# Fetches of a layer's first chunks wait for blocks of queries (graph transformer and message passing, one core)

## The chip, the cores and the metric

One core of one Trainium2 chip runs the whole program. The metric is the time of one execution on the device in microseconds; the median of three runs of the kernel before is 5631.02 us (5628.84 to 5631.04). The engines are PE (matrix products), DVE (vector), ACT (scalar functions), POOL (which here issues the indirect fetches) and SP (which issues plain transfers).

## The reference, cut to what matters

3125 nodes with 64 features, 100000 edges, sorted by destination. First four layers of attention along the edges, width 128, eight heads of 16:

```python
q = (h @ Wq.T + bq)[dst]; k = (h @ Wk.T + bk)[src]; v = (h @ Wv.T + bv)[src]   # per edge, 8 heads
alpha = sum(q * k) / 4                     # one number per edge and head
ex = exp(alpha - segment_max(alpha, dst)[dst])
out = segment_sum(ex / segment_sum(ex, dst)[dst] * v, dst)
h = layer_norm(gate(out, h @ Ws.T + bs) + h);  h = gelu(h @ W1.T + b1) @ W2.T + b2 + h
```

Then the result, added to x and normalised, goes through one stage of message passing: for every edge the products of x[src] and x[dst] and 16 radial functions of its length go through a small network, messages are summed by destination, and a second small network with a norm gives the output of 3125 x 64.

## The kernel before

**Nodes** are held in NB = 25 blocks of 128 rows, in NI = 5 groups of BW = 5 blocks. **Edges** are laid out in 806 places of 128 edges; a place belongs to one block of destinations. Sixteen places are a chunk (CH = 16), in four groups of four places (NG = 4, G = 4). There are 51 chunks in a pass; the last has 6 places. The fetched rows of a chunk lie in one of RING = 4 slots of SBUF, so that at most four chunks are fetched ahead. There are five passes over the edges: four layers and the message stage.

**A layer's head.** At the end of the layer in front (or in setup, for layer 0) PE and DVE make keys and values for all blocks (`keys` L953, `projected_keys` L1452, counted in `a_ev`), and SP writes them to the table `kv_table` in five transfers (`store_table` L389, counted in `tab_out`). Then PE makes queries: for each block one product of 128 x 256 and one transpose (`queries` L960, lines L966 and L970), and DVE evicts the block with a bias (L1464), which counts `q_ev` up by one; PE's product for block b waits for the eviction of block b - 2. ACT copies the transposes (L645). `begin_layer` (L1460) goes on, after the 25 evictions, with clearing the sums, one-hot matrices, the gate's sums over queries (L1476) and the products of queries and keys of chunk 0 (L1282, `multiply`).

**A chunk** is `attend_step` on PE (L854), ACT (L562) and DVE (L1328). In it the front of the next chunk is made: PE spreads terms (L797), ACT makes one-hot matrices of them (L547), PE picks the queries of the edges with these (L806), DVE multiplies them with the fetched keys (L1282) and sums per head (L1288), PE turns alpha (L843), DVE scans for the maximum (L1298, L1338). PE adds up weighted values (L825); its last product of a group counts `slot_free`, after which POOL may fetch into that group again.

**Fetches.** POOL runs `gather_chunk` for one chunk after the other. It waits for the table (`tab_out`), for the indices of the chunk (`idx_in`, loaded by SP, which in layer 0 waits for the reset rows before it loads those of chunk 4, L441), and for each group for `slot_free`, and issues one indirect transfer per place: 128 rows of 264 numbers (1056 bytes each). DVE waits on `kv_in[k][j]` for their landing. In layer 0 the fetches of slots 2 and 3 also wait for setup's transfers (L496, L498). POOL does nothing else in the passes, and its queue is in order: what waits holds everything behind it.

`START` is an offset that all counted semaphores begin with, so that waits have positive constants. `table is kv_table` is true in the four layers and false in the message stage. `q_ev` at START + NB * l + n means that n blocks of layer l's queries have been evicted.

Of the kernel before, what the change touches and what calls it, by code (L numbers as in the profile page):

```python
# [28 lines left out]
NB = -(-N // P)  # L29
# [10 lines left out]
NG = CH // G  # L40
# [16 lines left out]
START = (RING - 1) * NG + 1  # L57
# [19 lines left out]
def build_program(nc, a, out):  # L77
    with ExitStack() as ctx:
# [3 lines left out]
        def sem(name):  # L82
            return ctx.enter_context(nc.semaphore(name))
# [7 lines left out]
        kv_table = nc.dram_tensor("kv_table", [NPAD, KVW], F32, kind="Internal").ap()  # L91
# [158 lines left out]
        in_ps, in_act, s_ps, q_ev, h_ev = sem("in_ps"), sem("in_act"), sem("s_ps"), sem("q_ev"), sem("h_ev")  # L250
# [57 lines left out]
        def turn_of(l, i, k, j=0):  # L308

            return l * (FULL + (k < REM - 1 or (k == REM - 1 and j < LAST_NG))) + i  # L310
# [20 lines left out]
        def loaded(c, engine):  # L331

            _, values = nc.values_load_multi_w_load_instructions(  # L333
                place_blk[0:1, bass.ds(c * CH, CH)], [engine], min_val=0, max_val=NB - 1,
                skip_runtime_bounds_check_because="setup takes the minimum of every place's block and NB - 1, and counts from 0")
            return values
# [140 lines left out]
        @block.gpsimd  # L477
        def _(pool):


            for s in counted:
                pool.sem_inc(s, START)
            pool.wait_ge(su_idx, 1)
            for c in range(VC):
                pool.indirect_dma_start(row_sets[:, c, :], None, a["edge_t"],
                                        bass.IndirectOffsetOnAxis(ap=vti[:, c:c + 1], axis=0)).then_inc(su_rows, 16)
            uses = [[pool.alloc_register(f"uses{k}_{j}") for j in range(NG)] for k in range(RING)]
            for k in range(RING):
                for j in range(NG):
                    pool.reg_mov(uses[k][j], 0)  # L490

            def gather_chunk(k, turn, l, table, width, places=CH):
                groups = -(-places // G)
                used = [pool.snap(uses[k][j]) for j in range(groups)]
                if k == 2:
                    pool.wait_ge(su_termsd, 48)  # L496
                if k == 3:
                    pool.wait_ge(su_rstd, 16 * 2 * HEADS)  # L498
                pool.wait_ge(tab_out, 16 * NI * (l + 1))
                pool.wait_ge(idx_in[k], 16 * (turn + 1))  # L500
                for j in range(groups):
                    if isinstance(turn, int):
                        pool.wait_ge(slot_free[k][j], START + turn)
                    else:
                        pool.wait_ge(slot_free[k][j], START + used[j])
                        pool.reg_add(uses[k][j], uses[k][j], 1)
                    for t in range(j * G, min((j + 1) * G, places)):
                        pool.indirect_dma_start(slots[:, k, t, 0:width], None, table,  # L508
                                                bass.IndirectOffsetOnAxis(ap=idx[:, k, t:t + 1], axis=0))\
                            .then_inc(kv_in[k][j], 16)  # L510

            def gather_rest(l, table, width):
                for k in range(REM):
                    gather_chunk(k, turn_of(l, FULL, k), l, table, width, min(CH, PLACES - (RING * FULL + k) * CH))

            with pool.Fori(0, L) as l:
                with pool.Fori(0, FULL) as i:
                    for k in range(RING):
                        gather_chunk(k, turn_of(l, i, k), l, kv_table, KVW)
                gather_rest(l, kv_table, KVW)  # L520
            with pool.Fori(0, FULL) as i:
                for k in range(RING):
                    gather_chunk(k, turn_of(L, i, k), L, src_table, HID)
            gather_rest(L, src_table, HID)

            def root(sums, out, nth):

                pool.wait_ge(var_ans, START + 2 * nth)
                pool.tensor_tensor(guarded[:, :], sums, eps[:, :], ALU.add).then_inc(var_ans, 1)
                pool.wait_ge(var_ans, START + 2 * nth + 1)  # L530
                pool.tensor_tensor(out, guarded[:, :], half_power[:, :], ALU.pow).then_inc(var_ans, 1)

            pool.wait_ge(acc_done, START + CH * (L * CHUNKS + CHUNKS - 3))
            for i in range(NI):
                pool.memset(hidden[i][64:XW, :], 1.0).then_inc(hid_one, 1)
            for nth, (i, m) in enumerate(ASKED):
                pool.wait_ge(var_ready, START + nth + 1)
                root(var_of[2 * i + m], inv_of[2 * i + m], nth)
# [1271 lines left out]
```

## Time and profile before

| what | value |
|---|---|
| median of the timed runs | 5631.02 us (3 runs, 5628.84 to 5631.04) |
| span of the profiled execution | 7840.1 us |
| other time of the profiled execution | none is given beside its span |
| busy: PE, DVE, ACT, POOL | 4625.7, 4037.4, 2769.9, 3849.3 us |
| mean granted clock of PE | 0.679 of full speed |
| mean DMA rate | 68 GB/s over the span |

The span is the time from the first to the last instruction in the one execution that the hardware profiler recorded; it is 2209 us longer than the median of the timed runs. Durations and waits below are of that one execution. A wait is listed with what released it; "remote" means a releaser that the profile does not show, "issue" a stretch in which the engine waited for nothing that it shows.

### The profile page before, as it was taken

The numbers are of one execution on the slowest core, as the hardware profiler recorded it, in microseconds if no ns is written. First come the engines' busy times: TensorE is split into PE (matmuls) and PEld (weight loads), VectorE is DVE, ScalarE is ACT, GpSimd is POOL, SyncE is SP. The second block draws the span as 40 slices with busy tenths as digits, with TensorE's granted clock in tenths as the row PEclk, the third lists the DMA queues.
The fourth block names the chain that finished last, engine by engine and source line by source line (L and its number), as shares of the span: only waits on it lengthen the run. The fifth ranks groups of instructions, "written<-read, shape, count | busy, mean of one in ns | idle before, by whom it ended". The sixth has DMA issues, their size and how long they took to land.

```text
span 7840.1 us, 106032 instructions
## 1 busy us (share of the span) xinstructions
PE 4625.7 (59%) x22831; PEld 3727.9 (48%) x22832; DVE 4037.4 (51%) x11107; ACT 2769.9 (35%) x6493; POOL 3849.3 (49%) x4066
## 2 busy tenths in 40 slices
PE   4555555655556556555555565555555656666667
PEld 2444444534444445344444453444444545555555
DVE  4555555645555556455555565555555553333334
ACT  1333333423333334233333342333333432323333
POOL 3555555335555553345555543455555425555553
PEclk6666666676666666766666667666666677877887
DMA  5222222222322222222223222222322211111111
GB/s 127 78 79 76 77 76 78 52 66 73 79 78 77 78 80 56 69 67 79 76 78 79 78 62 69 68 78 77 80 78 79 60 33 43 44 44 44 44 44 30
DMA packets 267188, 536.13 MB, mean 68 GB/s; under 512 B 116253, under 2 KB 148689, under 8 KB 266509
## 3 DMA queue, kind: packets, MB, share of 16 engines
q0 software_dynamic: 180992, 490.24, 23.6%
q1 hardware_dynamic: 78901, 35.89, 1.9%
q10 hardware_dynamic: 6936, 6.69, 0.3%
q14 instruction: 314, 2.57, 0.1%
q8 instruction: 45, 0.74, 0.0%
HBM read 512.41 MB, written 18.03 MB: 68 GB/s over the span
## 4 chain that ended last, share of the span: by engine, by line
PE 26%; another core or an unknown queue 26%; issue 20%; DVE 17%; ACT 5%; DVEq 4%; ACTq 1%; SPq 0%; DMA 0%; POOL 0%; POOLq 0%
PE bank L806 9%; PE bank L825 7%; DVE acc L1265 6%; ACT oh L556 2%; DVEq L333 2%; PE bank L797 2%; PE bank L851 2%; PE bank L810 1%; DVE alpha L1288 1%; PE bank L879 1%; DVEq L1265 1%; DVE slots L1361 1%; DVE oh L1249 1%; PE bank L1001 1%
## 5 line engine op out<-in xcount | busy, mean ns | idle before, releaser
L508 POOL DMA_INDIRECT slots<-kv_table,idx x3224 | 3065.2, 951 | 3133.0 <-PE bank L825 1275.8
L825 PE MATMUL bank<-slots,oh 128*128 128x136 f32 (+1 forms) x8060 | 1593.0, 351 | 569.1 <-DVE acc L1265 506.4
L806 PE MATMUL bank<-qs,ohT 128*128 x8080 | 1685.7, 356 | 235.1 <-ACT ohT L547 129.2
L825 PEld LDWEIGHTS bank<-slots,oh 128*128 128x128 f32 x8060 | 1411.7, 252 | 704.7 <-DVE acc L1265 608.2
L806 PEld LDWEIGHTS bank<-qs,ohT 128*128 128x128 f32 x8080 | 1434.4, 257 | 456.6 <-issue 434.4
L1265 DVE TENSOR_TENSOR acc<-acc,bank 128x136 f32 (+1 forms) x4030 | 1172.0, 291 | 614.6 <-PE bank L825 171.5
L1282 DVE TENSOR_TENSOR slots<-slots,bank 128x512 f32<-128x512 f32 x808 | 551.8, 683 | 1322.6 <-remote 1291.5
L547 ACT ACTIVATE ohT<-bank,miss 128x512 f32<-128x512 f32 x1010 | 676.7, 683 | 1367.9 <-PE bank L797 1234.5
L508 POOL DMA_INDIRECT slots<-src_table,idx x806 | 760.4, 943 | 756.9 <-DMA idx<-src_e 247.9
L843 PE MATMUL bank<-ident,alpha 128*128 128x128 f32 x204 | 93.7, 459 | 1487.2 <-DVE alpha L1288 1481.7
L556 ACT ACTIVATE oh<-iota,rel_e 128x128 f32<-128x128 f32 x3168 | 962.8, 387 | 0.0
L843 PEld LDWEIGHTS bank<-ident,alpha 128*128 128x128 f32 x204 | 36.4, 178 | 1527.5 <-DVE alpha L1288 1521.6
L569 ACT COPY f_in<-bank 1x256 f32<-1x256 f32 x204 | 73.6, 361 | 1464.0 <-PE bank L851 723.1
L1361 DVE TENSOR_TENSOR slots<-slots,bank 128x544 f32<-128x544 f32 x808 | 575.9, 713 | 5.0
L1288 DVE TENSOR_REDUCE alpha<-slots 128x32 f32<-128x512 f32 x808 | 549.1, 680 | 0.6
L797 PE MATMUL bank<-terms,spread 12*128 12x512 bf16 x1010 | 519.8, 524 | 40.2 <-issue 32.8
L1416 DVE TENSOR_TENSOR slots<-slots,bank 128x512 f32<-128x512 f32 x202 | 138.4, 685 | 769.6 <-remote 426.3
L628 ACT ACTIVATE slots<-slots 128x512 f32<-128x512 f32 x202 | 127.1, 630 | 962.5 <-DVE slots L1416 915.4
L560 ACT ACTIVATE oh<-oh 128x1024 f32<-128x1024 f32 x396 | 418.4, 1057 | 12.8
L810 PE MATMUL bank<-resets 128*128 128x128 f32 x1616 | 403.5, 339 | 11.5 <-issue 11.3
L810 PEld LDWEIGHTS bank<-resets 128*128 128x128 f32 x1616 | 333.5, 254 | 9.6 <-issue 9.3
L879 PE MATMUL bank<-ident,ex 128*128 128x128 f32 x204 | 96.8, 474 | 257.9 <-ACT ex L586 249.2
(257 smaller groups left out, 4079.5 us busy)
## 6 DMA issues: line engine op xcount, KB each, us to landing
slots<-kv_table,idx POOLq DMA_INDIRECT x3224
kv_table<-slots SPq DMA_DIRECT2D x20, 660.0 KB, 3.4
slots<-src_table,idx POOLq DMA_INDIRECT x806
resets<-flat_len ACTq DMA_DIRECT2D x51, 128.0 KB
idx<-src_e SPq DMA_DIRECT2D x255, 8.0 KB
terms<-flat_rel SPq DMA_DIRECT2D x255, 12.0 KB
resets<-flat_rst SPq DMA_DIRECT2D x2, 1551.0 KB
w<-in_w SPq DMA_DIRECT2D x8, 256.0 KB
```

The costliest lines, as they stand in the source:

```text
L508: pool.indirect_dma_start(slots[:, k, t, 0:width], None, table, bass.IndirectOffsetOnAxis(ap=idx[:, k, t:t + 1], axis=0))\
L547: act.activation(ohT[:, j % 2, :, :].rearrange("p a b -> p (a b)"), bank[j % 2][:, :], ACT.Relu, bias=miss[:, 0:1], scale=-1.0).then_inc(o ...
L556: act.activation(oh[:, k % 2, t, :], iota[:, :], ACT.Abs, bias=rel_e[:, bass.ds((prior + 1) * CH + t, 1)], scale=-1.0).then_inc(oh_far, 1 ...
L560: act.activation(tiles, tiles, ACT.Relu, bias=1.0, scale=-1.0).then_inc(oh_made, 1 + skipped)
L797: pe.matmul(bank[j % 2][:, :], spread[:, j, :], terms[:, k, :], start=True, stop=True)\
L806: mm = pe.matmul(o, ohT[:, j % 2, t, :], qs[:, blocks[j * G + t], 0:HID], start=True, stop=basis is None)
L810: mm = pe.matmul(o, rbf[:, k % 2, half, :], m_1c[:, q, :], start=False, stop=True)
L825: mm = pe.matmul(bank[6 + part % 2][:, o:o + width], oh[:, k % 2, t, :], slots[:, k, t, HID:HID + width], start=True, stop=True)
L1265: dve.tensor_tensor(a_t, a_t, bank[6 + part % 2][:, o:o + width], ALU.add)\
L1282: dve.tensor_tensor(keys, keys, bank[2 + j % 2][:, :].rearrange("p (t k) -> p t k", t=G), ALU.mult).then_inc(spread_used, counts_for(j, gr ...
L1288: dve.tensor_reduce(alpha[:, :, j * G:(j + 1) * G].rearrange("p h t -> p t h"), slots[:, k, j * G:(j + 1) * G, 0:HID].rearrange("p t (h d) ...
L1361: dve.tensor_tensor(vals, vals, bcl(exs[:, j * G:(j + 1) * G, :], VW), ALU.mult).then_inc(w_done, counts_for(j, groups))
```

## The change

Two waits are put into POOL's `gather_chunk`, for the table of keys and values alone. In every chunk of slot 0 groups 1, 2 and 3 wait until 6, 12 and 18 blocks of the layer's queries have been evicted (group 0 does not). In every chunk of slots 1, 2 and 3 the first group waits for all 25. After a layer's head these counts are long passed; the waits are then executed but hold nothing. The message stage has none.

```diff
+            HEAD_STEP = NB // NG
+
             def gather_chunk(k, turn, l, table, width, places=CH):
...
                 for j in range(groups):
+                    if k == 0 and j > 0 and table is kv_table:
+                        pool.wait_ge(q_ev, START + NB * l + HEAD_STEP * j)
+                    if k > 0 and j == 0 and table is kv_table:
+                        pool.wait_ge(q_ev, START + NB * (l + 1))
                     if isinstance(turn, int):
                         pool.wait_ge(slot_free[k][j], START + turn)
```

## Rows read from the trace of the kernel before

**Rows 1.** The page: span, and busy time of each engine.
```profile
span 7840.1 us, 106032 instructions
...
PE 4625.7 (59%) x22831; PEld 3727.9 (48%) x22832; DVE 4037.4 (51%) x11107; ACT 2769.9 (35%) x6493; POOL 3849.3 (49%) x4066
```

**Rows 2.** Waits: engine, line, releaser: total us, times, longest.
```profile
DVE slots L1282 <- remote: 1291.5, 177, 8.1
...
POOL slots L508 <- DMA kv_table<-slots: 477.3, 3, 160.6
...
DVE slots L1416 <- remote: 426.3, 69, 28.1
...
DVE qs L1464 <- remote: 194.1, 34, 8.7
...
POOL slots L508 <- DMA src_table<-slots: 168.7, 1, 168.7
```

**Rows 3.** Timeline, POOL, layer 1's head: start, us busy, line [idle before <-releaser].
```profile
1651.74 0.94 POOL L508 DMA_INDIRECT slots<-kv_table,idx  x1 [157.38 <-DMA kv_table<-slots]
...
1730.48 0.95 POOL L508 DMA_INDIRECT slots<-kv_table,idx  x1 [0.30 <-issue]
```

**Rows 4.** Timeline, DVE, layer 1's head.
```profile
1658.91 0.42 DVE L1464 TENSOR_TENSOR qs<-bank,vec_qs 128x256 f32<-128x256 f32 x1 [1.01 <-PE bank L966]
...
1691.28 0.42 DVE L1464 TENSOR_TENSOR qs<-bank,vec_qs 128x256 f32<-128x256 f32 x1 [7.28 <-remote]
...
1741.72 0.76 DVE L1464 TENSOR_TENSOR qs<-bank,vec_qs 128x256 f32<-128x256 f32 x2 [2.39 <-PE bank L966]
...
1770.46 0.48 DVE L1338 TENSOR_TENSOR_SCAN fwd<-resets,icol,bank 128x128 f32<-128x128 f32 x1 [1.39 <-ACT icol L578]
```

**Rows 5.** Timeline, PE, the query product between two evictions of layer 1.
```profile
1684.05 1.22 PE L966 MATMUL bank<-w_qs,acc 128*128 128x256 f32 x2 [6.96 <-issue]
```

**Rows 6.** Timeline, PE, alpha's turns of two chunks of layer 0.
```profile
225.68 0.48 PE L843 MATMUL bank<-ident,alpha 128*128 128x128 f32 x1 [8.15 <-DVE alpha L1288]
...
253.10 0.47 PE L843 MATMUL bank<-ident,alpha 128*128 128x128 f32 x1 [8.23 <-DVE alpha L1288]
```

**Rows 7.** Timeline, PE and DVE, the end of layer 0.
```profile
1497.41 0.47 PE L843 MATMUL bank<-ident,alpha 128*128 128x128 f32 x1 [5.99 <-DVE alpha L1288]
...
1516.26 0.33 PE L843 MATMUL bank<-ident,alpha 128*128 128x128 f32 x1 [0.44 <-DVE alpha L1288]
...
1535.78 0.33 PE L843 MATMUL bank<-ident,alpha 128*128 128x128 f32 x1 [0.44 <-DVE alpha L1288]
...
1552.74 0.27 PE L843 MATMUL bank<-ident,alpha 128*128 128x128 f32 x1
...
1559.00 0.48 DVE L1338 TENSOR_TENSOR_SCAN fwd<-resets,icol,bank 128x128 f32<-128x128 bf16 x1 [0.88 <-issue]
```

**Rows 8.** Timeline, POOL, the last fetch of all.
```profile
7744.07 0.94 POOL L508 DMA_INDIRECT slots<-src_table,idx  x1 [0.30 <-issue]
```

**Rows 9.** Timeline, POOL and DVE, layer 0's head.
```profile
53.34 1.63 POOL L508 DMA_INDIRECT slots<-kv_table,idx  x1 [23.79 <-DMA idx<-src_e]
...
73.39 0.74 DVE L1464 TENSOR_TENSOR qs<-bank,vec_qs 128x256 f32<-128x256 f32 x2
...
78.32 0.42 DVE L1464 TENSOR_TENSOR qs<-bank,vec_qs 128x256 f32<-128x256 f32 x1 [0.64 <-issue]
...
134.38 0.95 POOL L508 DMA_INDIRECT slots<-kv_table,idx  x1 [0.30 <-issue]
...
151.31 0.97 DVE L1464 TENSOR_TENSOR qs<-bank,vec_qs 128x256 f32<-128x256 f32 x2 [0.24 <-PE bank L966]
...
177.96 0.48 DVE L1338 TENSOR_TENSOR_SCAN fwd<-resets,icol,bank 128x128 f32<-128x128 f32 x1 [1.64 <-ACT icol L578]
```

**Rows 10.** Windows: stretch, length, busy us of each engine, PE clock, DMA share, GB/s.
```profile
120.00:135.00 15.00, 2.87 (x6) 1.46 (x6) 0.85 (x2) 0.59 (x1) 11.34 (x13) 0.50 0.72 191
135.00:145.00 10.00, 1.63 (x4) 0.93 (x5) 0.85 (x2) 0.00 (x0) 0.32 (x1) 0.50 0.21 72
```

## The prediction

> **What bounds the kernel now.** I read the page first. Three engines are busy for about half of the span and none for all of it, and the span is 7840.1 us where the median of the timed runs is 5631.0 [rows 1]. So the traced execution carries some 2209 us that a timed one has not, and before anything is said of a layer's head it must be found where they sit. The waits show it: DVE's multiply of keys idles 1291.5 us in 177 waits, its last-stage sum 426.3 us and its query evictions 194.1 us, all for a releaser that the profile does not see [rows 2]. These three alone are 1912 us.
>
> The timeline of layer 1's head shows what they are. The table has landed at 1651.74 and POOL issues a fetch each 1.25 us, 64 in a row, the last at 1730.48 [rows 3]. Until 1658.91 eleven blocks of queries are evicted, one per 0.6 to 1.1 us. Then the gaps grow, to 7.28 us in front of 1691.28, and the 25th block is done at 1742.5, eleven us after the last fetch [rows 4]. PE has finished that block's work long before: its matmul starts 0.48 us after the eviction in front (1684.05, [rows 5]) and lasts 1.22 us, yet DVE starts the next only at 1691.28. So while POOL fetches without a pause, word from PE reaches DVE 6 us late. The same in the loop over chunks: PE stands for 8.2 us in front of alpha's turn, which waits for DVE's late multiply, and the turns are 27.4 us apart (225.68 to 253.10, [rows 6]). When POOL is silent the stall is gone: at the end of layer 0, chunks follow each other in 18.9 and 19.5 us (alpha's turns at 1497.41, 1516.26, 1535.78, [rows 7]), where the stretch with fetches had 27.4.
>
> Can a timed run have this stall? No, or hardly. 255 chunks at 27.4 us are 6987 us, more than the whole 5631. The fetches alone, five passes of 806, take 4030 x 1.25 = 5037 us (0.94 and a gap of 0.30 each, [rows 3]), 89% of the median, so in a timed run POOL fetches nearly always, and the chunks must still pass in less than 20 us each beside it.
>
> Now the timed run, worked out as if POOL set its pace. First fetch at 53.3; 5037 of fetches, and 2 more because the first 64 took 82.3 instead of 80 (53.34 to 135.6, [rows 9]); its idle time at three layer ends 477.3 [rows 2], before the last stage 168.7 [rows 2], after the last fetch 95 (7744.07 to the end, [rows 8]): 5834 us. Of each idle time a part goes when the chunks are close behind the fetches instead of three behind. The last chunk's alpha is turned at 1552.74 and the next table is there 99 us later [rows 3, 7]. With fetches setting the pace, chunk 49's last group is fetched 7.5 us before the last fetch ends, lands some 3 us later, and chunk 50's alpha comes 20 us after: -7.5 + 3 + 20 + 99 = 114.5 instead of the 158.3 traced, 44 less. If all five were alike: 5834 - 220 = 5614. That is 17 us, 0.3%, under the median; part of the 17 may lie around the span, for which the profile gives no time. So I take POOL's fetches as the bound of the timed runs, with DVE and PE close behind.
>
> How close? A layer by DVE's chain: last query 16 to 22 us after the table (eleven blocks by 1658.91, fourteen more at 0.61 to 1.07), 28 to the first full scan (1742.5 to 1770.46, [rows 4]), 50 chunks of 19.2 = 960, and 92.7 from chunk 50's scan at 1559.00 [rows 7] to the next table: 1097 to 1103. By POOL: 1007.5 + 114.5 = 1122. POOL is the later by about 20 us in layers 1 to 3.
>
> **The change part by part.** *The waits in layers 1 to 3.* Undisturbed, block 12 is there at about 1660, block 18 at 1663 to 1666, block 25 at 1667 to 1674. POOL comes to group 2 at 1661.7, to group 3 at 1666.7 and to chunk 1 at 1671.7 (8, 12 and 16 fetches behind 1651.74, [rows 3]). All waits have passed when POOL reaches them, or hold it for 2 us. I take 0. Bounds: in a timed run nothing; if the stall existed there too, the traced 80 us of head would shrink by up to 50, below.
>
> *The extra waits themselves.* 39 in chunks of slot 0 and 38 in the others, per layer, 308 in all. At a chunk's edge POOL already passes three waits with register sums, and the spacing stays 1.25 (the 64th fetch at 1730.48 is 63 x 1.25 behind the first, over three such edges, [rows 3]): the sequencer does them beside the fetch that is running. I take 0; bound from above 0.06 us each, a fifth of the 0.30 gap, 18 us.
>
> *Layer 0.* Here the waits do bite. The table is there at 53.34, but DVE is still in setup and evicts the first block at 73.39 and the sixth at 78.32 [rows 9]. Fetches 5 to 16 and chunks 1 to 3, which POOL issued in that time, now stand behind the waits. Group 0 as before; group 1 at 78.8 (block 6 done); group 2 at 83.8 to 85.1; group 3 at 88.8 to 91.5; chunk 1 at 93.8 to 99 (block 25 at 90 to 99), where it was at 75.6 (60 us before 135.6). Chunk 4's first fetch is ready after 48 x 1.25 = 60 us: 153.8 to 159. Before it was ready at 135.6, or, since its indices wait for the large reset rows whose transfer keeps DMA at 191 GB/s until 135, against 108 for the fetches' own 135 KB each 1.25 us, and then ends [rows 10], up to some 140.5. POOL is thus 13 to 23 us later, middle 18. From there 742 fetches are 927.5 and the tail 114.5: layer 0 ends by POOL at 1178 to 1183 before, 1196 to 1201 after.
>
> By DVE's chain: block 25 at 89 to 100, plus 25.7 to the first full scan (152.3 to 177.96, [rows 9]), plus 960, plus 92.7: 1167 to 1179 before and after. It lies just under POOL's path before, so not all of the 18 shows if the chunks are a little slower than 19.2; I take off 4. The sum: +14 us, all in layer 0, once. What hid the late queries before, a ring of 64 fetches made in advance, is what is spent.
>
> *What a quiet head gives back.* An eviction takes 0.42 us with fetches beside it and without [rows 4]; nothing to win there.
>
> A page speaks to the stall. The Trainium skill, "NOTIFIC — the notification-queue block", section 7.1 Overflow, says that the block's internal pipeline backpressures rather than lose a trace record, and that this can throttle an engine, though its authors saw no overflow. By that rule the stall belongs to traced executions alone, and a sum for timed runs has no gain at the head; without it, the gain of the second rival would be likelier. No row shows the mechanism; only the 7840 beside 5631 fits it.
>
> **Rivals.** *A, nothing shows (0.30).* If timed chunks take 19.6 us or more, DVE's chain ends layer 0 at 1187 to 1199 already, the late fetches hide behind it, and 2 to 9 us remain: 5636. For it: the two chains differ by 10 us in over 1100, and a 19.5 chunk stands in the rows. Against: PE ran partly at its lower clock in those chunks. That the waits never hold POOL is this case too, for layers 1 to 3.
>
> *B, the queries' stall is real in timed runs (0.20), the other side.* Place: blocks 12 to 25 of each layer. In the trace they took 84 us instead of 9 to 15; with the gating, POOL pauses after 8 to 12 fetches, PE's word comes through, and the last query is there 50 us earlier in the trace. In a timed run this pays only where it puts DVE's chain past POOL's, from 20 us of stall on in layers 1 to 3, and never more than what the median holds above POOL's own sum, 5631 - 5614 = 17, or about 30 if fetches are a little faster without the trace: 5615, at the best 5600. In the traced execution a gain of 10 to 50 us per layer is likely in any case, and proves nothing of the timed one.
>
> *C, the waits cost POOL (0.08).* 18 us on top of the forecast: 5663.
>
> **How the numbers follow.** Forecast (0.42): 5631 + 14 = 5645. A difference under 0.2%, 11 us, is taken as no change. Slower: most of the forecast (0.38), all of C, a little of A: 0.47. Same: A, and the edges of the forecast and of B: 0.34. Faster: B: 0.19. The range reaches down into B and up to C: 5605 to 5668; the forecast's own is 5636 to 5656.
>
> **What would show it.** In the changed trace: layer 0's fetch 5 at about 79 and fetch 17 at 94 to 99 or, with the stall, later; in layers 1 to 3 the last query 40 to 60 us earlier, and DVE's 194.1 us for queries down to a third; then more stalls in the first two chunks, since 48 fetches now run beside them. POOL's spacing must stay 1.25. Wrong would be: a median under 5620 (the stall was real), or spacing that grows at chunk edges (C), or no change of the median with a late fetch 17 (A).

## The result, and the profile after

| | median of runs | ratio, 95% interval |
|---|---|---|
| before | 5631.02 us (5628.27 to 5632.47, 7 runs) | |
| after | 5647.87 us (5644.12 to 5678.41, 7 runs) | 1.0038 (1.0029 to 1.0047) |

The changed kernel is slower by 17 us in the medians and by 16 to 26 us (21 in the middle) in the ratio; the forecast was 14 more, 5645, in a range of 5605 to 5668. One of the seven runs of the changed kernel took 5678.41 us, at a granted clock of 0.67 where the others had 0.76, and it is what lifts the ratio above the medians: without it the means differ by 16.7 us. The trace of the changed kernel has a span of 5646.1 us, 2 us under its median, so this one is a picture of a timed run, which the 7840.1 us of [rows 1] was not.

The page of the changed kernel. The lines are the span, the busy time of the engines, and the shares of the span in the chain of work that ended last.

```profile
span 5646.1 us, 106340 instructions
...
PE 4320.4 (77%) x22831; PEld 3525.4 (62%) x22832; DVE 4032.9 (71%) x11107; ACT 2775.2 (49%) x6493; POOL 3857.9 (68%) x4066
...
POOL 63%; issue 25%; PE 5%; DVE 4%; POOLq 2%; ACT 1%; DMA 1%; DVEq 0%; SPq 0%; ACTq 0%
```

DVE, ACT and POOL are as busy in us as in [rows 1] and PE is busy for 305 us less, at a mean granted clock of 0.763 instead of 0.679; the stretch that the work lies in is what is shorter. The chain is POOL's fetches, 63% by themselves and most of the 25% of "issue", the 0.30 us gap between two of them.

The waits of the changed kernel: engine, line, releaser, then total us, times, longest. They answer to [rows 2]; line numbers are 6 higher from L508 on.

```profile
POOL slots L514 <- DMA kv_table<-slots: 340.2, 3, 113.8
...
POOL slots L514 <- DMA src_table<-slots: 124.5, 1, 124.5
...
POOL slots L514 <- DVE qs L1470: 21.6, 8, 19.4
```

There is no idling of DVE for an unseen releaser any more. POOL's idle time at a layer's end is 113.8 where [rows 2] had 160.6, which is what the prediction worked out for chunks that follow close behind the fetches (114.5). The new wait, for evictions of queries, stands with 21.6 us, 19.4 of them once, in layer 0; the seven others are the usual gap of 0.30 us.

The timeline of POOL and DVE in layer 0's head, after; it answers to [rows 9].

```profile
53.00 1.62 POOL L514 DMA_INDIRECT slots<-kv_table,idx  x1 [23.49 <-DMA idx<-src_e]
...
78.03 0.94 POOL L514 DMA_INDIRECT slots<-kv_table,idx  x1 [19.44 <-DVE qs L1470]
...
93.05 0.95 POOL L514 DMA_INDIRECT slots<-kv_table,idx  x1 [0.30 <-issue]
...
153.19 0.95 POOL L514 DMA_INDIRECT slots<-kv_table,idx  x1 [0.30 <-issue]
...
1199.78 0.95 POOL L514 DMA_INDIRECT slots<-kv_table,idx  x1 [113.78 <-DMA kv_table<-slots]
```

Fetch 5 goes out at 78.03 (forecast 78.8), fetch 17 at 93.05 (93.8 to 99), fetch 65 at 153.19 (153.8 to 159), and layer 1 begins at 1199.78 (1196 to 1201). All fetches after the fifth run at 1.25 us without a hold until the layer is done: once late, POOL never makes it up. So only the wait for six blocks holds; the one for the 25th block, done at 88.80, has passed when POOL comes to fetch 17.

In layers 1 to 3 the waits stand at the same places. POOL's first rows of layer 2, after:

```profile
2326.34 0.95 POOL L514 DMA_INDIRECT slots<-kv_table,idx  x1 [113.83 <-DMA kv_table<-slots]
...
2330.11 0.95 POOL L514 DMA_INDIRECT slots<-kv_table,idx  x1 [0.30 <-DVE qs L1470]
...
2333.87 0.95 POOL L514 DMA_INDIRECT slots<-kv_table,idx  x1 [0.30 <-DVE qs L1470]
...
2337.63 0.94 POOL L514 DMA_INDIRECT slots<-kv_table,idx  x1 [0.30 <-DVE qs L1470]
```

A query's eviction stands as the releaser, but of fetches 4, 7 and 10, in front of which the change has no wait (it has them before fetches 5, 9, 13 and 17), and the gap is the usual 0.30: nothing was waited for.

### The profile page after: what moved, and what is told of

Its sections match the earlier page's. It is cut to its first block, busy times and chain, and to the rows that moved or that the text cites. A ratio compares the mean times of both kernels' runs of the same rounds, so it can differ in the third digit from the quotient of the medians.

```text
span 5646.1 us, 106340 instructions
## 1 busy us (share of the span) xinstructions
PE 4320.4 (77%) x22831; PEld 3525.4 (62%) x22832; DVE 4032.9 (71%) x11107; ACT 2775.2 (49%) x6493; POOL 3857.9 (68%) x4066
## 4 chain that ended last, share of the span: by engine, by line
POOL 63%; issue 25%; PE 5%; DVE 4%; POOLq 2%; ACT 1%; DMA 1%; DVEq 0%; SPq 0%; ACTq 0%
POOL slots L514 63%; PE bank L1007 1%; PE bank L964 1%; PE bank L996 1%; PE bank L972 1%; POOLq L512 1%; DVE acc L1271 1%; POOLq L511 0%; DVE slots L1518 0%; POOLq L496 0%; DVE slots L1524 0%; DVE slots L1522 0%; POOLq L502 0%; DVE slots L1464 0%; DMA slots<-kv_table,idx 0%
## 5 line engine op out<-in xcount | busy, mean ns | idle before, releaser
L831 PE MATMUL bank<-slots,oh 128*128 128x136 f32 (+1 forms) x8060 | 1517.4, 338 | 320.7 <-DVE acc L1271 317.9
L812 PE MATMUL bank<-qs,ohT 128*128 x8080 | 1633.0, 348 | 106.3 <-DVE slots L1288 36.3
L831 PEld LDWEIGHTS bank<-slots,oh 128*128 128x128 f32 x8060 | 1338.0, 240 | 438.9 <-DVE acc L1271 398.8
L812 PEld LDWEIGHTS bank<-qs,ohT 128*128 128x128 f32 x8080 | 1385.4, 250 | 305.9 <-issue 283.7
L803 PE MATMUL bank<-terms,spread 12*128 12x512 bf16 x1010 | 485.1, 489 | 66.5 <-issue 57.2
L816 PE MATMUL bank<-resets 128*128 128x128 f32 x1616 | 364.4, 313 | 0.0
L816 PEld LDWEIGHTS bank<-resets 128*128 128x128 f32 x1616 | 298.5, 230 | 0.0
L1344 DVE TENSOR_TENSOR_SCAN fwd<-resets,icol,bank 128x128 f32<-128x128 f32 (+1 forms) x204 | 97.9, 480 | 243.0 <-issue 237.4
L857 PE MATMUL bank<-ident,fwd 128*1 128x128 f32 x204 | 64.8, 317 | 243.2 <-DVE bwd L1306 211.1
L885 PEld LDWEIGHTS bank<-ident,ex 128*128 128x128 f32 x204 | 37.0, 181 | 342.4 <-ACT ex L592 342.4
```

The lines of the kernel that those rows point to most:

```text
L803: pe.matmul(bank[j % 2][:, :], spread[:, j, :], terms[:, k, :], start=True, stop=True)\
L812: mm = pe.matmul(o, ohT[:, j % 2, t, :], qs[:, blocks[j * G + t], 0:HID], start=True, stop=basis is None)
L816: mm = pe.matmul(o, rbf[:, k % 2, half, :], m_1c[:, q, :], start=False, stop=True)
L831: mm = pe.matmul(bank[6 + part % 2][:, o:o + width], oh[:, k % 2, t, :], slots[:, k, t, HID:HID + width], start=True, stop=True)
```

## The experiments

The theory: POOL's fetches set the pace of a timed run, and the loss is how much later fetch 17 of layer 0 goes out, one for one, once. Its rivals: A, DVE's chain of chunks is level with POOL's and hides lateness; B, evictions of queries stall beside fetches in timed runs too; C, each executed wait costs POOL time. The runs came in three groups (e0 to e3; e4 to e7; e8 and e9), the first two on one chip and the third on another. The kernel before has medians of 5618.68, 5617.63 and 5618.01 us in them, 13 us less than in the result. Each difference is against the median of its own group. The times expected of e0 to e3 were counted from 5631, so that they all lie 10 to 12 us too high; what is compared is the differences.

| run | what | median us | difference | ratio, 95% interval |
|---|---|---|---|---|
| e0 | kernel before | 5619.45 | +0.8 | 1.0000 (0.9991 to 1.0009) |
| e1 | waits in layer 0 alone | 5637.31 | +18.6 | 1.0032 (1.0019 to 1.0044) |
| e2 | waits in layers 1 to 3 alone | 5621.28 | +2.6 | 1.0002 (0.9993 to 1.0011) |
| e3 | 1232 waits that never hold | 5619.26 | +0.6 | 1.0001 (0.9992 to 1.0010) |
| e4 | slot 0's waits alone | 5634.80 | +17.2 | 1.0031 (1.0020 to 1.0041) |
| e5 | waits for the last query alone | 5633.67 | +16.0 | 1.0027 (1.0016 to 1.0037) |
| e6 | chunk 1 of layer 0 held longer | 5653.05 | +35.4 | 1.0064 (1.0050 to 1.0078) |
| e7 | DVE's head 14.7 us longer | 5625.24 | +7.6 | 1.0012 (1.0003 to 1.0021) |
| e8 | setup: sources first | 5619.80 | +1.8 | 1.0004 (0.9995 to 1.0013) |
| e9 | the whole change | 5637.53 | +19.5 | 1.0035 (1.0021 to 1.0049) |

### e0: the kernel before, a second trace

No edit.

> The kernel before, unchanged, for a second trace. Theory (fetches by POOL set the pace, the late word from PE is a thing of the one trace of 7840 us): 5631 us within 3; a trace that is free of the late word has a span near 5631, the 25th query of layer 0 at about 89 us and of layers 1 to 3 within 25 us of the table, fetch 65 of layer 0 at 135 to 141. Rival (the stall of queries is real whenever fetches run beside them): also 5631, but each layer's last query again some 90 us after the table.

Its span is 5617.9 us. (The trace of [rows 1] is of an execution slower than any timed one; nothing of its 2209 us is in this one.) Lines of e0's waits, then DVE and POOL at layer 0's and layer 1's head:

```profile
POOL slots L508 <- DMA kv_table<-slots: 338.8, 3, 114.4
...
DVE slots L1282 <- DMA slots<-kv_table,idx: 74.9, 80, 1.8
...
DVE qs L1464 <- PE bank L966: 26.3, 56, 4.4
```

```profile
75.73 0.95 POOL L508 DMA_INDIRECT slots<-kv_table,idx  x1 [0.30 <-issue]
...
88.93 0.42 DVE L1464 TENSOR_TENSOR qs<-bank,vec_qs 128x256 f32<-128x256 f32 x1 [0.25 <-PE bank L966]
...
115.12 0.48 DVE L1338 TENSOR_TENSOR_SCAN fwd<-resets,icol,bank 128x128 f32<-128x128 f32 x1 [1.64 <-ACT icol L578]
...
135.74 0.95 POOL L508 DMA_INDIRECT slots<-kv_table,idx  x1 [0.30 <-issue]
...
939.48 0.69 DVE L1282 TENSOR_TENSOR slots<-slots,bank 128x512 f32<-128x512 f32 x1 [1.57 <-DMA slots<-kv_table,idx]
...
1179.97 0.94 POOL L508 DMA_INDIRECT slots<-kv_table,idx  x1 [114.38 <-DMA kv_table<-slots]
...
1194.90 0.42 DVE L1464 TENSOR_TENSOR qs<-bank,vec_qs 128x256 f32<-128x256 f32 x1 [0.25 <-PE bank L966]
...
1223.78 0.48 DVE L1338 TENSOR_TENSOR_SCAN fwd<-resets,icol,bank 128x128 f32<-128x128 f32 x1 [1.31 <-ACT icol L578]
...
5567.31 0.94 POOL L508 DMA_INDIRECT slots<-src_table,idx  x1 [0.30 <-issue]
```

The gaps of 7 to 8 us in front of evictions [rows 4] are gone, though fetches run beside them all the time: the last query of layer 1 is done 15 us after the table. DVE's waits for keys are now for the fetched rows themselves, which is what a kernel paced by its fetches looks like. In layer 0 this is so only late: the wait in front of 939.48 is the first of seven in the layer. Until then DVE works off the lead of the ring. The two chains are nearly level. Rival B has nothing left to give back: in layer 0 the 25 evictions take 16.4 us with sixteen and more fetches beside them (e0, the last done at 89.3) and 16.4 us with few (after, 88.8; it began 0.6 earlier). Fetch 17 goes out at 75.73 and fetch 65 at 135.74, so the change's lateness of fetch 65 is 153.19 - 135.74 = 17.5 us.

### e1 and e2: the waits in layer 0 alone, and in the others alone

POOL's layer 0 is written out ahead of a loop over layers 1 to 3, and a flag `gated` says where the waits stand; e1:

```diff
-            with pool.Fori(0, L) as l:
+            with pool.Fori(0, FULL) as i:
+                for k in range(RING):
+                    gather_chunk(k, turn_of(0, i, k), 0, kv_table, KVW, gated=True)
+            gather_rest(0, kv_table, KVW, True)
+            with pool.Fori(1, L) as l:
                 with pool.Fori(0, FULL) as i:
                     for k in range(RING):
-                        gather_chunk(k, turn_of(l, i, k), l, kv_table, KVW)
-                gather_rest(l, kv_table, KVW)
+                        gather_chunk(k, turn_of(l, i, k), l, kv_table, KVW, gated=False)
+                gather_rest(l, kv_table, KVW, False)
```

In e2 the two flags are the other way round. In both, the waits for `slot_free` of the written-out layer count by register, as those of the loop do.

> The waits stand in layer 0 alone; POOL's program for layer 0 is written out ahead of the loop over layers 1 to 3. Theory: all of the loss, 5648 us (plus 14 to 20 on the kernel before). Rival C (each executed wait costs POOL some 0.055 us, 308 of them the 17 us): 77 waits, 5635. Rival (the waits of layers 1 to 3 hold POOL): 5631 to 5636.

> The waits stand in layers 1 to 3 alone, with the same written-out layer 0 but without waits there. Theory: they have passed when POOL comes to them, 5631 us within 4. Rival C: 231 waits, 5644. Rival B (a stall of queries that costs in timed runs): below 5631, down to 5615.

e1 costs 18.6 us, as much as the whole change (e9: 19.5, measured in another group); e2 costs 2.6 us with an interval around nothing (-4 to +6). The loss is layer 0's. Both also say that writing layer 0 out costs nothing that can be measured.

### e3: waits that never hold

```diff
-                        pool.wait_ge(q_ev, START + NB * l + HEAD_STEP * j)
+                        for _ in range(4):
+                            pool.wait_ge(q_ev, START + NB * l)
...
-                        pool.wait_ge(q_ev, START + NB * (l + 1))
+                        for _ in range(4):
+                            pool.wait_ge(q_ev, START + NB * l)
```

> At each of the change's places stand four waits on the same semaphore for a value that was passed before the table of the layer was there, 1232 executed in all; none ever holds. Theory: the sequencer does them beside the running fetch, 5631 us within 4, spacing of fetches 1.25 us. Rival C: 4 x 17 = 68 us more, 5699.

0.6 us for 1232 waits; rival C wanted 68. The fetches' group of lines, e3 (line, count, busy us, mean ns, then idle us before them by what ended it) and below it e0's:

```profile
L516 POOL DMA_INDIRECT slots<-kv_table,idx x3224 | 3063.7, 950 | 1346.6 <-issue 978.7 <-DMA kv_table<-slots 341.5 <-DMA idx<-src_e 23.9
```

```profile
L508 POOL DMA_INDIRECT slots<-kv_table,idx x3224 | 3062.9, 950 | 1343.4 <-issue 980.6 <-DMA kv_table<-slots 338.8 <-DMA idx<-src_e 24.0
```

The idle time put down to "issue" is the same 0.30 us for each fetch with three or four waits at a chunk's edge (e0) or with seven or eight (e3, slots 1 to 3).

### e4 and e5: either kind of wait alone

```diff
-                    if k > 0 and j == 0 and table is kv_table:
-                        pool.wait_ge(q_ev, START + NB * (l + 1))
```

That is e4; e5 takes out the other two lines instead.

> Only the waits of slot 0 (6, 12, 18 blocks) stay; chunks 1 to 3 do not wait for the last query. Theory (the loss is how late fetch 17 of layer 0 is, one for one): group 1 at 78, fetch 17 at 93 as with the whole change, 17 us over the kernel before. Rival (the wait for the last query is what costs): at most 4 us over it.

> Only the wait of slots 1 to 3 for the last query stays. Theory: chunk 0 is fetched from 53 to 75, fetch 17 goes out at the 25th query, 89.3, instead of 75.6: 14 us over the kernel before, some 4 less than the whole change. Rival (the two kinds of waits add up): the whole change less that of e4, near 0.

e4 costs 17.2, e5 16.0 us, and together (e9: 19.5) they cost, within the intervals, no more than either: they are two lines for one hold. In the whole change only e4's line holds POOL; e5 shows that the other would, were it alone. POOL's rows in layer 0, e4 and then e5:

```profile
78.67 0.94 POOL L512 DMA_INDIRECT slots<-kv_table,idx  x1 [19.48 <-DVE qs L1468]
...
153.81 0.94 POOL L512 DMA_INDIRECT slots<-kv_table,idx  x1 [0.30 <-issue]
...
1197.71 0.94 POOL L512 DMA_INDIRECT slots<-kv_table,idx  x1 [113.87 <-DMA kv_table<-slots]
```

```profile
91.32 0.94 POOL L512 DMA_INDIRECT slots<-kv_table,idx  x1 [16.51 <-DVE qs L1468]
...
1196.59 0.95 POOL L512 DMA_INDIRECT slots<-kv_table,idx  x1 [114.68 <-DMA kv_table<-slots]
```

In e5 the hold stands directly in front of fetch 17: it goes out at 91.32, two us later than expected, 15.6 after e0's; the next layer begins 1196.59 - 1179.97 = 16.6 later, the median is 16.0 more. In e4, with fetch 17 some 18 us late, it is 17.7 and 17.2.

### e6: a longer hold

On e1's form, with no wait of the change left:

```diff
+                    if k == 1 and j == 0 and gated:
+                        pool.wait_ge(alpha_turned, START + 1)
```

> None of the change's waits; instead chunk 1 of layer 0 alone waits for the turned alpha of chunk 0, about 108, some 32 us later than 75.6. Theory: 32 us over the kernel before, 1 us per us. Rival A (DVE's chain of chunks ends the layer nearly as late and hides lateness): clearly less than the hold, by 10 us or more.

```profile
109.61 0.94 POOL L512 DMA_INDIRECT slots<-kv_table,idx  x1 [34.05 <-PE bank L851]
...
1212.22 0.95 POOL L512 DMA_INDIRECT slots<-kv_table,idx  x1 [112.13 <-DMA kv_table<-slots]
```

Fetch 17 is 33.9 us later than in e0, the next layer begins 32.3 later, the median is 35.4 more (28 to 44 by the ratio). With e5 and e4 that is a line of three points, 16, 18 and 34 us of lateness, and 16.0, 17.2 and 35.4 of loss. By the traces, 16.6, 17.7 and 32.3: of a hold in layer 0 nothing is hidden that stands out from the 2 us by which these differ.

### e7: DVE's chain made later, POOL untouched

```diff
+                for n in range(4):
+                    dve.memset(acc[:, :, :], 0.0).then_inc(spin, 1)
+                    dve.wait_ge(spin, 4 * l + n + 1)
                 dve.memset(acc[:, :, :], 0.0).then_inc(acc_zero, 1)
```

> The kernel before, with four more clearings of the sums on DVE in each layer's head, each waited for, 4 x 2.9 = 12 us later for DVE's chain in each of four layers; POOL is not touched. Theory (DVE's chain has 12 us to spare in layer 0 and 20 in the others): 0 to 3 us over the kernel before. Rival A (DVE's chain is the bound or level with it): 24 to 48 us over it.

Neither number was hit: 7.6 us (2 to 12 by the ratio), of four times 14.7 (a clearing with its wait takes 3.67, not 2.9). Rows of e7:

```profile
128.95 0.48 DVE L1338 TENSOR_TENSOR_SCAN fwd<-resets,icol,bank 128x128 f32<-128x128 f32 x1 [1.59 <-ACT icol L578]
...
137.18 0.94 POOL L508 DMA_INDIRECT slots<-kv_table,idx  x1 [2.82 <-DMA idx<-src_e]
...
1094.84 0.48 DVE L1338 TENSOR_TENSOR_SCAN fwd<-resets,icol,bank 128x128 f32<-128x128 bf16 x1 [0.88 <-issue]
...
1188.04 0.94 POOL L508 DMA_INDIRECT slots<-kv_table,idx  x1 [120.85 <-DMA kv_table<-slots]
...
2311.21 0.94 POOL L508 DMA_INDIRECT slots<-kv_table,idx  x1 [113.40 <-DMA kv_table<-slots]
```

Layer 1 begins at 1188.04, 8.1 us later than in e0, and POOL's idle time there is 120.85 instead of 114.38: in layer 0 DVE's chain has become the later one. It never waits for fetched rows there (no wait of L1282 for `kv_table` in the layer, seven in e0), and its 50 chunks take 19.3 us each (128.95 to 1094.84), where sixteen fetches of POOL take 20.1 (e0: 1.2536 us each). From layer 1 to layer 2 pass 1123.2 us, in e0 1124.0: there the 14.7 us are hidden whole. So DVE's chain of layer 0 takes 1188.04 - 128.95 = 1059.1 us from its first full scan; in e0 it would end at 115.12 + 1059.1 = 1174.2, and POOL's ends at 1180.0. It had 6 us to spare in e0, not 12, and in layer 1, by the same length, 1223.78 + 1059.1 = 2282.9 against 2303.98: 21. The cause of the 8.1 us is read off these rows, of one length of delay. That fetch 65 itself goes out 1.4 us later, held for its indices, is too little for it: POOL stands idle 6.5 us longer at the layer's end.

### e8: fetches that begin earlier

In setup DVE takes over the seven blocks of sources before it converts the destinations:

```diff
-            step(dve.tensor_copy(rows_f, rows_d))
-            for c in range(VC):
-                ins = dve.tensor_scalar(r_rel[:, c, :], rows_f[:, c, :], vt[:, 1, c:c + 1], None, ALU.subtract)
-            ins.then_inc(su_turn, 1)
             for k in range(VC):
                 take(k)
+            step(dve.tensor_copy(rows_f, rows_d))
+            for c in range(VC):
+                ins = dve.tensor_scalar(r_rel[:, c, :], rows_f[:, c, :], vt[:, 1, c:c + 1], None, ALU.subtract)
+            ins.then_inc(su_turn, 1)
```

> The kernel before, with one reordering in setup: the seven blocks of sources are taken over before the destinations are converted, so that the indices are loaded and POOL's first fetch goes out some 2.3 us earlier (51.0 instead of 53.35). Theory (POOL's fetches set the pace from the first on, one for one): fetch 65 at 133.4 and the first layer's end 2.3 us earlier in the trace; in the median 1 to 4 us less, hardly to be told from the kernel before. Rival (its lead is lost later, the reset rows or DVE's chain): fetch 65 at 135 or later and the layer's end unmoved.

```profile
51.24 1.32 POOL L508 DMA_INDIRECT slots<-kv_table,idx  x1 [21.59 <-DMA idx<-src_e]
...
117.27 0.48 DVE L1338 TENSOR_TENSOR_SCAN fwd<-resets,icol,bank 128x128 f32<-128x128 f32 x1 [1.52 <-ACT icol L578]
...
136.57 0.94 POOL L508 DMA_INDIRECT slots<-kv_table,idx  x1 [3.30 <-DMA idx<-src_e]
...
1182.54 0.94 POOL L508 DMA_INDIRECT slots<-kv_table,idx  x1 [116.23 <-DMA kv_table<-slots]
```

The first fetch goes out 2.1 us earlier, but fetch 65 waits 3.30 us for chunk 4's indices and the layer ends 2.6 us later than in e0. The rival is right here: by the program SP loads those indices only behind the large reset rows, and they are there at 136 to 137 (e2, e7 and e8 wait for them), when POOL comes to fetch 65 (135.74 without a wait in e0). Fetch 65 is only 0.8 us later than in e0; the other 1.8 us of the layer's end lie behind the last fetch (116.23 instead of 114.38), and what made them is not shown. DVE's first full scan is 2.2 us later too (117.27), as its setup was put off. In this kernel lateness of the fetches costs one for one; earliness is not paid for. I had no version that is faster than the kernel before.

### e9: the whole change again

No edit to the changed kernel.

> The whole change again, on the chip of e8. Theory: 17 to 18 us over the kernel before, as e1 and e4; fetch 17 of layer 0 at 93, next table 17 to 18 us after that of the kernel before.

```profile
93.92 0.95 POOL L514 DMA_INDIRECT slots<-kv_table,idx  x1 [0.31 <-issue]
...
1198.37 0.94 POOL L514 DMA_INDIRECT slots<-kv_table,idx  x1 [114.04 <-DMA kv_table<-slots]
```

Fetch 17 is 18.2 us later than in e0 (which ran on the other chip), the next layer begins 18.4 us later, the median is 19.5 more (12 to 28 by the ratio).

## Why the prediction was right

**The stall of the first trace is not in timed runs.** Right: argued from 255 x 27.4 us being more than the median, shown by e0.

**POOL's fetches set the pace.** Right. The sum for such a run was 5614; e0's span is 5617.9. Its terms: idle time at layer ends 114.5, measured 114.4, 113.2 and 111.3; before the last stage 168.7 - 44 = 124.7, measured 125.5; after the last fetch 95 - 44 = 51, measured 49.7. So near a hit has some luck in it: the 4030 fetches with their gaps took 5050.6 us where the sum had 5039, 12 more, and the five stretches at the ends took 514 where it had 521. (The 158.3 from which the 44 was taken runs from the start of the last fetch; the idle time is 157.4 in [rows 3], 1 us less.) The 17 us between the sum and the median of 5631 were thought to lie in part around the span; there are 1.9 (5619.79 for an execution with a span of 5617.9). The rest is the 13 us between the groups of runs, below.

**Waits in layers 1 to 3: 0.** Right (e2). The last query is done 15 us after the table in e0, where the forecast had 16 to 22 and POOL comes to chunk 1 at 20. It is no wide margin at every wait: in e9 fetch 5 of layer 1, at 1203.78, has a gap of 0.74 us instead of the usual 0.30, and in e2 the longest is 0.9.

**The executed waits: 0.** Right (e3).

**A quiet head gives nothing back.** Right (16.4 us for the queries of layer 0 in either kernel). The gain of 10 to 50 us per layer that was thought likely in a traced execution was not seen, since the traces since then have no stall to take away.

**Layer 0, lateness 13 to 23, middle 18.** Right: 17.5 in the first trace after, 18.2 in e9. (By the end of the layer the first is 19.8 late, since its fetches run 1.2576 us apart instead of 1.2536; e9 is 18.4 late.) PE's queries ran at the 0.61 us spacing early, which put the hold at the lower end; fetch 65 of the kernel before was at 135.74, also the lower end of its 135.6 to 140.5.

**Less 4 for DVE's chain.** This is the term that was mis-sized. The chain was put at 1167 to 1179 with POOL at 1178 to 1183, and part of the lateness was thought to hide in their overlap, which by these bounds is 1 us; the 4 was worked out from no row. The chain ends at 1174 with POOL at 1180 (e7), so nothing hides, and e4, e5 and e6 lose all of their hold. Without the 4 the forecast would have been 18 us of loss and 5649; measured are 17 in the result and 19.5 in e9, and 5647.9. The chain was also said to be the same before and after. It is not: the fetches of chunk 0 that are held make DVE wait for them, and its first full scan is 3.5 us later after (6.1 in e9) than in e0's 115.12. By the length read from e7 it still ends some 20 us ahead of POOL, so this costs nothing.

```profile
118.65 0.48 DVE L1344 TENSOR_TENSOR_SCAN fwd<-resets,icol,bank 128x128 f32<-128x128 f32 x1 [1.57 <-ACT icol L584]
```

**Rivals.** A (2 to 9 us) falls with e6 and e7, though by 6 us of room only; B with e0 and e2; C with e3. How little it takes for A is an estimate from e7's figures: with chunks of 19.7 us instead of 19.3 DVE's chain would end layer 0 at 1194 in the kernel before, and only a few us of the loss would be left.

What stays open: what delayed PE's word in the execution of 7840 us. Of twelve traces here it is in that one alone, so that tracing by itself does not bring it about. The page of the Trainium skill that the prediction cites ("NOTIFIC — the notification-queue block", section 7.1) says that the notification path can throttle an engine. No run here can show whether it did.

## What to carry to other kernels

Set the traced span beside the timed median before a stall in the trace is acted on: this one's stall filled a quarter of the span and did not exist in what was timed. A queue that works without a pause from the first table to the last result may be the bound even where the profile shows it half idle; count its instructions, multiply by their spacing, and compare with the median. A wait put into such a queue cost all of its hold here, once, where it held (layer 0), and nothing that could be measured where it had passed. Before the loss is put down as one for one, ask how far ahead of the queue the next chain ends: here it was 6 us in the first layer.

## What was not expected of the hardware

The same program had one traced execution of 7840.1 us and another of 5617.9 us. In the slow one what PE signalled reached DVE some 6 us late in stretches with fetches [rows 4, 5], though not from the first fetch on: with fetches going out since 53.34, the evictions up to 78.32 have gaps of at most 1 us in front of them. The durations of the instructions themselves were the same (a fetch 951 and 950 ns on the mean, an eviction of queries 0.42 us).

The kernel before has 5631.02 us in the result and 5618 in all three groups of experiments, on two chips: 13 us, nearly as much as the change costs, so that only comparisons inside a group tell anything here. The cause is open. The length of a fetch varies with the execution: its mean is 952 ns in the trace after and in that of e1, 950 in those of e0 and e9, and over 4030 fetches 2 ns are 8 us; e1's traced execution took 5649.6 us, 12 above its own median.
